# Shared groups of weights split in the last attention step, routed turns and gathers begun in the shared block, routed stores awaited later, gathered rows summed early

## What is computed

```python
# attention, in chunks of 128 tokens, 16 heads of 32, weights rounded to -1, 0, 1 times a scale
scores = einsum('bhtd,bhsd,hts->bhts', q, k, mask)          # mask: decay, lower triangle
o      = scale * (einsum(scores, v) + einsum(q, lam_t, S))  # S: state carried from chunk to chunk
S      = lam_T * S + einsum(k, lam_rev, v)
out    = rmsnorm(rmsnorm(o)) @ quant(proj_w).T
# experts, for all 4096 tokens
shared = (silu(g) * u) @ w_sh_down        # g, u = split(x @ w_sh_gate_up), 1024 wide
routed = sum over the 2 best of 8 experts of weight * ((silu(g_e) * u_e) @ w_down[e])   # 256 wide
```

## Time and profile before

| | us |
|---|---|
| median of 3 runs | 1270.86 (1269.21 to 1272.81) |
| the profiled execution, its own time | 1270.78 |
| its span, first to last instruction | 1269.0 |
| PE busy | 1203.0 (95%) |
| DVE, ACT, POOL busy | 661.0, 476.3, 490.1 |
| granted PE clock, mean | 0.986 |

### The profile page before, as it was taken

How to read it: one execution, slowest core, us unless ns; L and a number is a source line. 1 busy time by engine, 2 the same in 40 slices (tenths; PEclk the granted TensorE clock), 3 DMA queues, 4 the chain that set the end, 5 groups by cost and what they waited for, 6 DMA issues and landing times. The chain is left out here.

```text
span 1269.0 us, 29255 instructions
## 1 busy us (share of the span) xinstructions
PE 1203.0 (95%) x10768; PEld 815.1 (64%) x10768; DVE 661.0 (52%) x1410; ACT 476.3 (38%) x1030; POOL 490.1 (39%) x432
## 2 busy tenths in 40 slices
PE   4899999999999679999999799999999899999997
PEld 3676777677677357777777344444444477777775
DVE  7888889989998578533333222222222223333333
ACT  6454555555555353322222233333333311111111
POOL 3456656765666200454501122222222044444444
PEclk8999999999999889999999899999999999999999
DMA  6598988788788764334324577887788434444444
GB/s 208 134 254 190 211 234 224 203 224 242 202 218 239 203 202 158 97 105 100 100 100 59 152 184 190 190 198 188 195 193 193 96 133 150 150 149 149 150 150 134
DMA packets 269373, 217.40 MB, mean 171 GB/s; under 512 B 196784, under 2 KB 203056, under 8 KB 269296
## 3 DMA queue, kind: packets, MB, share of 16 engines
q1 hardware_dynamic: 255344, 180.03, 52.9%
q0 software_dynamic: 12848, 35.47, 9.8%
q10 hardware_dynamic: 1104, 0.81, 0.2%
HBM read 115.97 MB, written 56.51 MB: 136 GB/s over the span
## 5 line engine op out<-in xcount | busy, mean ns | idle before, releaser
L570 PE MATMUL sc<-x,WG 128*128 128x256 f16 x3072 | 349.2, 274 | 11.8 <-DVE WD L1780 6.9
L570 PEld LDWEIGHTS sc<-x,WG 128*128 128x128 f16 x3072 | 302.0, 98 | 62.2 <-DVE WD L1780 7.1
L1499 PE MATMUL sc<-WG,raw 128*128 x852 | 209.3, 382 | 6.0 <-DMA raw<-raw 3.7
L1918 DVE SCALAR_TENSOR_TENSOR actv<-sc,up_inv,sg 128x512 f32<-128x512 f32 x64 | 48.0, 750 | 247.2 <-ACT sg L1756 238.0
L1483 POOL DMA_INDIRECT raw<-xs_dram,slots x71 | 67.3, 948 | 281.5 <-DMA raw<-raw 209.3
L1756 ACT ACTIVATE sg<-sc,gate_inv 128x512 f32<-128x512 f32 x64 | 44.0, 687 | 308.8 <-PE sc L570 249.2
L1506 PE MATMUL yp<-WD,ah 128*128 128x512 f16 x512 | 152.3, 379 | 0.7 <-DVE al L1923 0.7
L1499 PEld LDWEIGHTS sc<-WG,raw 128*128 128x128 f16 x852 | 83.9, 98 | 92.4 <-issue 9.1
L1986 POOL DMA_INDIRECT raw<-y_dram,gidx x64 | 64.2, 1004 | 151.8 <-DVE ys L1899 102.3
L839 PE MATMUL ring<-WG 128*128 128x256 f16 x1024 | 119.6, 273 | 2.4 <-PEq L241 2.0
L2123 DVE TENSOR_TENSOR alr<-rat,ahr 128x256 f16<-128x256 f32 x71 | 30.1, 424 | 158.6 <-ACT ahr L2100 151.0
(11 more groups left out here) (260 smaller groups left out, 1778.3 us busy)
## 6 DMA issues: line engine op xcount, KB each, us to landing
y_dram<-raw SPq DMA_DIRECT2D x71, 256.0 KB
WG<-in_L_attn_x SPq DMA_DIRECT2D x32, 512.0 KB, 5.3
WG<-in_L_ffn_w_gate_up SPq DMA_DIRECT2D x16, 512.0 KB, 4.7
xs_dram<-WG SPq DMA_DIRECT2D x16, 512.0 KB, 3.7
xT_dram<-x SPq DMA_DIRECT2D x16, 512.0 KB, 2.7
x_dram<-x SPq DMA_DIRECT2D x32, 256.0 KB, 2.1
x<-xT_dram SPq DMA_DIRECT2D x16, 512.0 KB
x1s<-x_dram SPq DMA_DIRECT2D x16, 512.0 KB
```

Source lines behind the costliest of these rows:

```text
L570: ins = pe.matmul(gu[:, h, f * 2 * P:(f + 1) * 2 * P].rearrange("p (u t) -> p u t", u=2), w[:, kk, b, part * P:(part + 1) * P], x[:, :, a ...
L1499: ins = pe.matmul(gu[bank], x(kk, a), w[:, 0, kk, b, :], start=(i == 0), stop=(i == len(done) - 1))
L1918: v.scalar_tensor_tensor(out=actv[:, g % 2], in0=gu[g % 2][:, 1].rearrange("p (f t) -> p f t", f=FT), scalar=up_inv[:, 1:2], in1=sg[:], op ...
```

## The change

The change has five parts.

- **Maxima a step earlier.** The first two 16ths of the weights are loaded during setup; `weight_maxima` of chunk 0 is done in the prologue and that of chunk n+1 in step n. `weight_scales` is done in the last step but one (index 14): `top_maxima`, `joined_maxima` and `weight_scales` on DVE, `turn_maxima` and `spread_maxima` on PE.
- **Splits in the last attention step.** SP loads groups 1 and 0 and the tokens `x16` in step 14, before that step's `load_xr` and `turn_y`; in step 15 it loads group 2 between `turn_y(0)` and `turn_y(1)`, and group 3 behind `turn_y(1)`. ACT and DVE have an order of their own for step 15 (`last_step`) with the splits of groups 0 to 2 (ACT: to 3) between their attention work; PE runs `gate_up` of group 0 ahead of `proj(0)` and that of group 1 behind `proj(1)`. Silu, product and remainder of group 0 are made there as well. The shared block begins with `down` of group 0.
- **Routed turns and gathers.** All four first turns (before: two) and eight gathers (before: four) are issued in the shared block; two turned tiles get memory of their own (`xh_more`), and both first expert numbers are read there. The shared block no longer waits for its last stores at its end; the routed block does.
- **Routed end.** The last tile runs a quarter of `gate_up` before `down` and three quarters behind it, and the wait for the last `y_dram` stores goes to POOL in the next block.
- **End.** `add_gathered` adds the gathered rows to `x1` in group 3 of each step, so that `token_outputs` is one operation per row block; the stores of the first half's rows go ahead of those of the second.

```diff
@@ SP, attention step
-                    sp.wait_ge(S["wmax_ready"], n)
-                    load_weights(*after(q, par))
-                else:
-                    for g in range(2):
-                        load_group(sp, k, g)
-                    sp.wait_ge(S["logits_ready"], NCH)
+                if norm:
+                    sp.wait_ge(S["wmax_ready"], n + 1)
+                    load_weights(q + 1, par)
+                elif front:
+                    load_group(sp, k, 1)
+                    sp.wait_ge(S["hl_ready"], 2 * NCH)
+                    load_group(sp, k, 0)
+                    sp.wait_ge(S["logits_ready"], NCH - 1)
                     sp.wait_ge(xT_out[0], 16 * (NCH // 2))
                     sp.dma_start(x16[:, 0], xT_dram[0]).then_inc(x_ins[0][0], 16)
                 sp.wait_ge(S["x1_ready"], 2 * n)
                 load_xr(q, par)
                 for u in range(B):
                     turn_y(u, q, par)
+                    if not front:
+                        sp.wait_ge(split, PIECES * (u + 1))
+                        load_group(sp, k, u + 2)
@@ PE, attention step
                     project("v0", *nxt, st)
+                    if not norm:
+                        turn_maxima()
                     scores(0, *nxt)
                 else:
-                    all_maxima()
+                    pe.wait_ge(split, KT)
+                    pe.wait_ge(x_ins[0][0], 16)
+                    gate_up(pe, sc[:, 0:2], x16[:, 0], WG[:, 0]).then_inc(gu_fulls[0], 1)
                 proj(0, q, par, st)
                 if front:
                     outer(1, q, par, st)
                     project("v1", *nxt, st)
+                    if not norm:
+                        spread_maxima()
                 proj(1, q, par, st)
             run_steps(pe, prologue, step)
-            pe.wait_ge(split, KT)
-            pe.wait_ge(x_ins[0][0], 16)
-            gate_up(pe, sc[:, 0:2], x16[:, 0], WG[:, 0]).then_inc(gu_fulls[0], 1)
+            pe.wait_ge(split, PIECES + KT)
+            gate_up(pe, sc[:, 2:4], x16[:, 0], WG[:, 1]).then_inc(gu_fulls[0], 1)
@@ DVE, attention: prologue and last step
                 h_low(0, 1)
+                weight_maxima(0, 0, (1, 2, 3))
+                weight_maxima(0, 0, (0,))
+            def last_step(q, par):
+                decayed_scores(1, q, par)
+                v.wait_ge(S["wscale_ready"], 1)
+                low_group(0, range(0, 3))
+                o_mean(0, q, par)
+                low_group(0, range(3, 4))
+                normed(0, q, par)
+                low_group(0, range(4, PIECES))
+                o_mean(1, q, par)
+                normed(1, q, par)
+                y_low(0, q, par)
+                low_group(1, range(0, 3))
+                y_low(1, q, par)
+                low_group(1, range(3, PIECES))
...
+                v.wait_ge(UNIT["sg_ready"][0], 1)
...
+                residual(0, q, par, st)
...
+                residual(1, q, par, st)
+                low_group(2, range(PIECES))
@@ ACT, last step
+                high_group(0, range(PIECES))
+                take_oT(0, q, par, st)
+                o_square(0, q, par)
+                o_root(0, q, par)
+                take_oT(1, q, par, st)
+                high_group(1, range(0, 1))
+                o_square(1, q, par)
+                high_group(1, range(1, 2))
+                o_root(1, q, par)
+                y_high(0, q, par)
+                high_group(1, range(2, 4))
+                on_squares(0, q, par)
+                y_high(1, q, par)
+                on_squares(1, q, par)
+                high_group(1, range(4, PIECES))
...
+                act.activation(sg[:], sc[:, 0].rearrange("p (f t) -> p f t", f=FT), ACT.Silu,
...
+                high_group(2, range(2, PIECES))
+                high_group(3, range(PIECES))
@@ SP, last shared step of the first half
-                                for r in range(2):
+                                for r in range(XH):
                                     turn(sp, r, S["sp_passed"])
...
                     if half == 0:
                         sp.wait_ge(slot_in, 16)
+                        return
@@ POOL
-                        for r in range(XG):
+                        for r in range(2 * XG):
+                            if r >= XG:
+                                pool.wait_ge(turned[r - XG], 16)
                             gather(pool, r)
@@ PE, last routed tile
-                            gate_up(pe, gu_whole[0], xT[:, 0], WG[:, 0]).then_inc(gu_fulls[1], 1)
+                            gate_up(pe, gu_whole[0], xT[:, 0], WG[:, 0], (0,))
...
                         down(pe, yp[par], (ah[:, par], al[:, par]), WD[:, own], True, True).then_inc(S["y_full"], 1)
+                        if last:
+                            gate_up(pe, gu_whole[0], xT[:, 0], WG[:, 0], (1, 2, 3)).then_inc(gu_fulls[1], 1)
@@ DVE, second half
-                                v.tensor_tensor(ys[:, u], ys[:, u], gy[:, u, 0], ALU.add).then_inc(S["ysum_ready"], 1)
-                                v.tensor_tensor(ys[:, u], ys[:, u], gy[:, u, 1], ALU.add).then_inc(S["own_ready"], 1)
+                            if half == 1 and g == GROUPS - 1:
+                                add_gathered(q, par)
```

333 lines of the change are left out of this document (182 added, 151 removed).

## The result

The changed kernel took 1263.1 us (median of 11 runs, 1254.4 to 1269.4) beside 1272.8 for the kernel before on the same chip (11 runs, 1267.2 to 1278.5). The ratio is 0.9924, with a 95% interval of 0.9901 to 0.9947: faster by about 0.8%, 9.7 us, where 18.4 had been predicted. The profiled execution took 1262.65 us, with a span of 1260.9 us against 1269.0.

A forecast was written before the change was run, and what follows sets the result against it. PE bounds the kernel, busy 1203.0 of 1269.0 us, so only its idle time, low clock and the end can pay. +2.2 - 5.8 - 8.2 - 4.1 - 2.5 = -18.4 gives 1252.4 us; 8-in-10 range 1241 to 1260.

The forecast's parts named there:

- part 3: Attention step 15 up to the barrier: 29.4 us instead of 44.0; together with Part 2, -5.8 us.
- part 4: Border from first shared to routed block: waits and low clock go, -8.2 us, bounds -4 and -8.6.
- Part 2: Attention step 14: first turn lands behind 4.2 MB of loads, PE idles 5.8 us; about +8.4 us, bounds +0.8 and +11.
- The first rival: Steps 14 and 15: the queue doesn't hold turns back, waits shrink to 0.8 + 0.5 us, total 1241 us; chance 0.16.
- the barrier that belongs to PE: End of attention step 15: PE is the last engine to reach the barrier, by 0.6 us only.
- The second wait: Shared to routed border: PE's 3.74 us wait for a turned tile and 2.4 us of low clock behind it would go.
- Parts 5 and 6: Routed to shared border: idle time and low clock go, -4.1 us; kernel's end: last store goes out earlier, -2.5 us.
- Part 1: Prologue: chunk 0's maxima on DVE stand ahead of the first step's masked scores; +2.2 us, bounds 0 and 2.8.
- the 0.66 us of cover: Prologue: time between DVE's masked scores (57.74) and PE taking them up (58.40), covering part of 2.8 us of maxima.

The follow-up runs named there:

- Experiment 3: Changed kernel with step 14's loads (groups 0 and 1, turned x) issued behind its turns; ratio to the kernel before 0.989 (0.986 to 0.992).
- experiment 5: Changed kernel with step 14's two group loads on ACT's DMA queue and the turned x behind the turns; executed once, 1267.96 us.
- experiment 2: Changed kernel with both turns of step 15 issued ahead of group 2's load; ratio to the kernel before 0.9958 (0.9924 to 0.9992).
- Experiment 1: Changed kernel with the gathers of slot tiles 4 to 7 put back into the routed block; ratio to the kernel before 0.987 (0.979 to 0.995).
- experiment 4: Changed kernel with chunk 0's prologue maxima over an eighth of the data; outputs of step 1 at 83.33 us, 2.8 us later than in the changed kernel.
- experiments 9 and 10: Changed kernel without early sum, 1265.1 us against 1269.3; changed kernel with second shared block's gathers held, 1263.1 and 1272.6 us on two chips against 1265.2 and 1267.4.

## Why the prediction was right or wrong

The direction and the cost that the change brings with it were right; the gain came out at half, below the range. What failed were the length of one load in part 3 (2.6 us), the barrier in part 4 (3.0 us), and waits inside the routed block that no part had (3.3 us). Point by point:

- **Part 2 was right, term by term.** It gave a wait of 5.8 us (5.76 measured) and 8.4 us in all (8.2). Experiment 3 takes the wait and 7.5 us away by moving the loads alone. The first rival, that turns aren't held, is refuted. The prediction took the order of SP's queue for the reason ("a turn seems to land only after what was issued earlier"). In the changed kernel each late turn did land 1.0 us behind the last load ahead of it; experiment 5 shows that loads on another queue delay a turn too, by 1.7 us there, and leaves open whether they hold it as long.
- **Part 3 failed in one term:** "Group 2's load (1.6 MB; about 5.9 us from issue to landing, an estimate from the same rate)". It took 8.6 us, from 445.81 to 454.40, and the turn landed 1.0 behind it, so PE idled 5.83 us and not 3.2. That is 2.6 us. The rate of 307 GB/s was that of long transfers in a busy stretch; these 1.6 MB moved at 183 GB/s with their start counted. In experiment 2 the same load, with no turn behind it, took 7.9 us, and the next 1.6 MB landed 4.5 us later, so 2.0 of the 2.7 us by which the load was mis-sized are there whenever it has to start on an empty queue, and 0.7 only with the turn behind it. The rest of the part held: the waits before the turns (0.76 and 1.24), 1.78 against 1.8 ahead of the first projection, the barrier that belongs to PE. The Silu began 0.01 us behind its table load here too, so the drain of the Trainium skill (ScalarE: Activation LUTs, What ACT_TABLE_LOAD costs) shows in neither trace.
- **Part 4 failed in one term:** "0.3 to 0.4 stays for the barrier". 3.38 stayed, 3.0 us more. The prediction counted which store and which turn the barrier no longer waits for, but not that POOL drains there too and now issues its last gather 10 us later. Experiment 1 shows it. The second wait and its low clock went as forecast.
- **Parts 5 and 6 were right:** the border 0.32 us, the table's -10.4 holds 4.1 for it and 6.3 for part 4's second wait, and the missing 3.6 us are the two waits inside the routed block (3.3); the end -2.9 for -2.5. "In the other steps the additions lie beside PE's 5.2 us of `gate_up`" held in the profiled run; on three chips the early sum came with gaps in PE that no part had (experiments 9 and 10).
- **Part 1 was half right.** 0.9 to 1.0 us are the maxima's (experiment 4), 2.2 were forecast. The step that failed is the 0.66 us of cover: it was taken up to PE's matmuls at 58.40, which don't read the masked scores; those that do began at 59.49, so 1.75 us were covered. What the pair shows beyond, up to 3.7 us by step 14, is mostly the spread of attention itself: the outputs of step 14 began between 395.0 and 402.4 us in the 18 traces of changed kernels (mean 399.2) and at 397.8 and 399.1 in the two of the kernel before.
- **The routed waits** were in no part. 17 of 18 changed traces have one to three of them, 0.2 to 4.1 us in sum; the two traces of before have none beyond the wait for the second tile (3.74 and 3.86), which part 4 took away. Experiment 1, with the gathers where they were, has them as well, so they are not the early gathers'. Their cause was not found.

The misses of the table's rows, 1.5 - 0.2 + 2.3 + 0.5 + 3.0 + 3.6 - 0.4 = 10.3, are the distance between -18.4 and the profiled -8.1. And the measured 9.7 us was itself on the good side: on three more chips the change had ratios of 0.9963, 0.9958 and 0.9953, 4 to 6.5 us.

## What to carry to other kernels

Before a transfer on which PE depends within microseconds, add up everything that is in flight, in its own queue above all, and count a short load at its own issue-to-landing time rather than at a long stretch's rate; then ask what becomes last once it is moved, since each fix here uncovered another wait. At a block's end list every engine's last instruction, with those that only issue gathers: one issued early for the next block can hold the end of this one. And read a change of less than 1% from stretches of several traces on several chips, because one pair showed 3.7 us in a place worth 0.9.

## What the runs showed of the hardware that was not expected

- POOL's drain at a block's end lasted until 6.9 to 7.6 us after its last gather was issued (7.5 with four gathers, 6.9 with eight), while DVE's took 0.8.
- A transposing transfer moved its first packet 1.2 us after its issue with nothing in flight, and 2.0 us after it while another queue's loads filled the DMA engines; behind 4.2 MB on its own queue it took 10.0 us to land instead of 3.1. Six 512 KB loads issued by ACT held that engine for 5.0 us.
- With the early sum, the second shared block took 240.78 us in every trace on three chips and 245 to 251 on three others, by gaps of 0.1 to 1 us in four to seven of its eight steps, released by nothing visible, all of them (over 0.15 us) while packets of POOL's gathers moved.
- A low clock followed PE's waits of 5 to 8 us in all traces; waits of 3.2 to 3.6 us at the routed border, and of 2 to 3 us elsewhere, were followed by one in some and not in others.
